# GNN message sending: casts as transpositions, wide picks, and one PSUM pool of 8 banks

## The reference

```python
msgs = edge_vals[:, None] * x[edge_col]              # x is layer-normed here
agg = segment_sum(msgs, edge_row, num_segments=n)
h = (1.0 + eps) * x + agg
h = bn_relu(h @ W1 + b1); h = bn_relu(h @ W2 + b2)   # batch norm over the nodes
x = x + h
H = gelu(layernorm(x) @ W1f + b1f)
probs = softmax(H @ Wg + bg); e = argmax(probs)
out = x + probs[e] * (H @ Wd[e] + bd[e])             # one expert per node
```

## Time and profile before

| | |
|---|---|
| three runs, median (lowest to highest) | 3251.73 us (3246.09 to 3256.91) |
| the profiled execution's own time | 3250.25 us |
| its span | 3248.4 us |
| mean granted clock of TensorE | 0.956 of 2.4 GHz |
| busy, share of the span | PE 88%, PEld 74%, DVE 74%, ACT 50%, POOL 25% |
| DMA | 710.52 MB, mean 219 GB/s |

### The profile page before, as it was taken

The page is one execution under the profiler, slowest core; times in us unless marked ns, Lnnn a source line. Parts: engine busy times, 40 slices in busy tenths (PEclk is TensorE's granted clock), DMA queues, the critical chain, the costliest instruction groups (busy, mean ns, idle before and its releaser), DMA issues. The chain is left out here.

```text
span 3248.4 us, 70401 instructions
## 1 busy us (share of the span) xinstructions
PE 2860.7 (88%) x20204; PEld 2392.9 (74%) x20205; DVE 2408.5 (74%) x5908; ACT 1618.7 (50%) x3203; POOL 823.2 (25%) x885
## 2 busy tenths in 40 slices
PE   4887678888888887999999999987999999599998
PEld 2333477777777776888888888755777777499998
DVE  8998967677777765888888888766666666666665
ACT  3664456566666663222222222575777777533332
POOL 4221045555555552000000000021222222122222
PEclk9888889999999998999999999998999999799999
DMA  2332077778777777999999999100344444566664
GB/s 56 106 115 74 20 261 291 279 283 306 290 292 283 284 288 298 330 335 333 345 332 327 333 329 332 49 0 26 131 157 178 155 174 159 215 211 211 214 214 135
DMA packets 214806, 710.52 MB, mean 219 GB/s; under 512 B 28495, under 2 KB 104313, under 8 KB 189514
## 3 DMA queue, kind: packets, MB, share of 16 engines
q1 hardware_dynamic: 130778, 405.55, 36.7%
q0 software_dynamic: 83952, 304.02, 24.1%
HBM read 383.91 MB, written 340.05 MB: 223 GB/s over the span
## 5 line engine op out<-in xcount | busy, mean ns | idle before, releaser
L1437 PE MATMUL coll_ps_sum<-coll_rows,coll_hot 128*128 128x256 f32 x2940 | 657.4, 380 | 23.5 <-DVE coll_hot L1372 23.2
L1088 PE MATMUL send_ps_msg<-send_parts,send_pick 128*128 128x256 f32 x3584 | 558.6, 300 | 108.1 <-ACT send_msg L1128 86.6
L1437 PEld LDWEIGHTS coll_ps_sum<-coll_rows,coll_hot 128*128 128x128 f32 x2940 | 550.1, 190 | 101.5 <-DVE coll_hot L1372 28.3
L1088 PEld LDWEIGHTS send_ps_msg<-send_parts,send_pick 128*128 128x128 f32 x3584 | 476.3, 198 | 129.8 <-DVE send_pick L991 78.3
L943 POOL DMA_INDIRECT messages<-send_msg,send_to x448 | 468.9, 1047 | 379.9 <-ACT send_msg L1128 235.9
L1128 ACT ACTIVATE send_msg<-send_ps_msg 128x1024 f32<-128x1024 f32 x448 | 454.1, 1027 | 221.7 <-PE send_ps_msg L1088 158.3
L991 DVE TENSOR_SCALAR send_pick<-send_ps_local,edges_down 128x512 fp32r<-128x512 f32 x448 | 334.2, 746 | 209.5 <-PE send_ps_local L1076 136.4
L1372 DVE TENSOR_SCALAR coll_hot<-coll_nodes,coll_rows 128x128 f32<-128x128 f32 x1470 | 393.4, 340 | 2.2 <-DMA coll_rows<-messages 0.8
L1491 ACT ACTIVATE nodes_hid<-coll_ps_turned 128x256 f32 (+1 forms) x98 | 37.5, 383 | 553.1 <-PE coll_ps_turned L1269 553.1
L1566 POOL CAST lin_x_hi<-lin_hT 128x1024 fp32r<-128x1024 f32 x25 | 29.2, 1168 | 940.1 <-ACT lin_hT L1702 887.4
L2033 DVE TENSOR_TENSOR gate_act_lo<-gate_act_h,gate_act_hi 128x512 fp32r<-128x512 f32 x200 | 141.7, 709 | 167.5 <-ACT gate_act_hi L1942 126.3
(11 more groups left out here) (335 smaller groups left out, 5887.2 us busy)
## 6 DMA issues: line engine op xcount, KB each, us to landing
coll_rows<-messages SPq DMA_DIRECT2D x98, 1300.0 KB, 7.3
coll_rows<-messages SPq DMA_DIRECT2D x98, 1170.0 KB, 7.3
exp_pay<-regions SPq DMA_DIRECT2D x105, 646.0 KB
send_window<-node_rows SPq DMA_DIRECT2D x112, 128.0 KB
node_rows<-sort_xn SPq DMA_DIRECT2D x25, 512.0 KB, 5.0
coll_own<-node_rows SPq DMA_DIRECT2D x98, 128.0 KB, 4.1
sort_xt<-in_x_dram SPq DMA_DIRECT2D x24, 512.0 KB, 4.3
layers_w<-in_x_dram SPq DMA_DIRECT2D x24, 384.0 KB
```

The costliest lines, as they stand in the source:

```text
L1088: ins = pe.matmul(ps_msg[:, q % 2, a, :], pick[:, q * RUN + a, :], parts[:, s % 2, part, :], start=(part == 0), stop=(part == 1))
L1437: ins = pe.matmul(ps_sum[:, s, 0:D], hot_of(s, j), features(u, j), start=(j == CX), stop=(j == CJ - 1))
```

## The change

Per group, TensorE no longer turns `local`; each of the 16 casts is a transposition of one column of `local`, repeated 128 times by a step of 0, in bf16, 8 to a call and one call to a bank. `pick` has two buffers and is made by two instructions of 1024 elements instead of four of 512. All of PSUM is one tensor of 8 banks; products, casts and sorted columns take them in turn. The order changes: sort and take run for group i+3, rows and slots for i+4. `parts` and `local` have 4 slots. localT, its clearing, ps_turned and their semaphores go.

```diff
-        pick = m.sb("pick", [P, QJ, P], F32R)
+        local = m.sb("local", [P, SLOTS, QJ], BF16)
+        pick = m.sb("pick", [P, 2, QJ, P], F32R)
-        parts = m.sb("parts", [P, 2, 2, D], F32R)
+        parts = m.sb("parts", [P, SLOTS, 2, D], F32R)
-        ps_found = m.ps("ps_found", [P, 512])
-        ps_turned = m.ps("ps_turned", [P, 512])
-        ps_local = m.ps("ps_local", [P, 2, RUN, P])
-        ps_msg = m.ps("ps_msg", [P, 2, RUN, D])
+        banks = m.ps("banks", [P, 8, 512])
+        PAIR_OF = (0, 4, 6, 2)
+        CAST_AT = (2, 0)
+        SORT_AT = 3
+        def bank(g, at):
+            return (4 * (g % 2) + at) % 8
+        def sums_of(s, q):
+            return banks[:, bank(s, PAIR_OF[q]):bank(s, PAIR_OF[q]) + 2, :].rearrange("p b (a f) -> p (b a) f", f=D)
+        def casts_of(s, h):
+            return banks[:, bank(s + 1, CAST_AT[h]), :].bitcast(BF16).rearrange("p (j m) -> p j m", m=P)
+        def found_of(u, first):
+            return banks[:, first if first is not None else bank(u + 1, SORT_AT), 0:SORTED]
...
+                def picks(i, s, h):
+                    if later(i, 2):
+                        dve.wait_ge(gathered, QS * (i - 1))
+                    dve.wait_ge(cast_done, 2 * i + h + 1)
+                    dve.tensor_scalar(pick[:, s % 2, h * QJ // 2:(h + 1) * QJ // 2, :], casts_of(s, h), k.down[:, 0:1], None,
                                       ALU.is_equal).then_inc(pick_ready, 1)
...
                 def group(i, s, turn):          # VectorE
+                        rest(i + 1, (s + 1) % SLOTS)
+                        rows_of(i + 4, s % 2)
+                        picks(i + 1, (s + 1) % SLOTS, 0)
+                        slots_of(i + 4, s % 2)
                         meta(i + 2, far, far % 2, turn if s + 2 < SLOTS else turn + 1)
+                        picks(i + 1, (s + 1) % SLOTS, 1)
...
+                def sort(i, s, first=None):
-                    if later(i, 1):
-                        pe.wait_ge(found_ready, i)
+                    if later(i, 4):
+                        pe.wait_ge(kept, QS * (i - 3) - 1)
+                def cast(i, s, h):
+                    if h == 0:
+                        pe.wait_ge(local_ready, i + 1)
+                    if later(i, 2):
+                        pe.wait_ge(kept, QS * (i - 1) - 1 if h == 0 else QS * (i - 1) + 1)
+                    elif later(i, 1) and h == 1:
+                        pe.wait_ge(kept, 1)
+                    for j in range(QJ // 2):
+                        n = h * QJ // 2 + j
+                        ins = pe.transpose(casts_of(s, h)[:, j, :], local[:, s, n:n + 1].to_broadcast([P, P]), k.ident16[:])
                 def gather(i, s, q):
                     if q == 0:
                         pe.wait_ge(rest_ready, i + 1)
+                        pe.wait_ge(pick_ready, 2 * i + 1)
+                        if later(i, 1):
+                            pe.wait_ge(kept, QS * i - 2)
+                        else:
+                            pe.wait_ge(found_ready, 2)
+                    if q == 1:
+                        pe.wait_ge(pick_ready, 2 * i + 2)
+                    if q == 2:
+                        if later(i, 1):
+                            pe.wait_ge(kept, QS * i)
+                        else:
+                            pe.wait_ge(found_ready, 3)
+                    if q == 3:
+                        if comes(i, 1):
+                            pe.wait_ge(pick_ready, 2 * i + 3)
+                        if comes(i, 3):
+                            pe.wait_ge(found_ready, i + 4)
...
                 def group(i, s, turn):          # TensorE
                     gather(i, s, 0)
+                        cast(i + 1, (s + 1) % SLOTS, 0)
+                        sort(i + 3, (s + 3) % SLOTS)
                     gather(i, s, 1)
                     gather(i, s, 2)
+                        cast(i + 1, (s + 1) % SLOTS, 1)
                     gather(i, s, 3)
...
-                    act.activation(localT[0:QJ, d, :], ps_turned[0:QJ, 0:P], ACT.Copy).then_inc(localT_ready, 1)
                 def group(i, s, turn):          # ScalarE
                         high(i + 1, (s + 1) % SLOTS, turn if s + 1 < SLOTS else turn + 1)
                     keep(i, s, turn, 0)
+                        take(i + 3, (s + 3) % SLOTS)
                     keep(i, s, turn, 1)
                     keep(i, s, turn, 2)
-                        take_turned(i + 2, s % 2)
                     keep(i, s, turn, 3)
```

More of the change, by code:

```diff
@@ L1009, in rest @@
                     dve.wait_ge(high_ready, i + 1)
-                    dve.tensor_tensor(parts[:, s % 2, 1, :], window[:, s, :], parts[:, s % 2, 0, :].bitcast(F32),
+                    dve.tensor_tensor(parts[:, s, 1, :], window[:, s, :], parts[:, s, 0, :].bitcast(F32),
                                       ALU.subtract).then_inc(rest_ready, 1)
@@ L1015, in group @@
                     steps.restart()
-                    near, far = (s + 1) % SLOTS, (s + 2) % SLOTS
+                    far = (s + 2) % SLOTS
                     if comes(i, 1):
[L1018 to L1021, removed]
+                        rest(i + 1, (s + 1) % SLOTS)
+                    if comes(i, 4):
+                        rows_of(i + 4, s % 2)
                     if comes(i, 1):
[L1023 to L1027, removed]
+                        picks(i + 1, (s + 1) % SLOTS, 0)
+                    if comes(i, 4):
+                        slots_of(i + 4, s % 2)
                     if comes(i, 2):
@@ L1036, in _ @@
                 meta(0, 0, 0, 0)
-                rest(0, 0)
[L1038 to L1044, removed]
+                picks(0, 0, 0)
+                picks(0, 0, 1)
+                rows_of(2, 0)
+                slots_of(2, 0)
+                meta(1, 1, 1, 0)
+                rest(0, 0)
+                rows_of(3, 1)
+                slots_of(3, 1)
                 all_groups(dve, group)
@@ L1082, in gather @@
                         pe.wait_ge(rest_ready, i + 1)
-                    pe.wait_ge(pick_ready, QS * i + q + 1)
-                    if q >= 2 or later(i, 1):
-                        pe.wait_ge(kept, QS * i + q - 1)
+                        pe.wait_ge(pick_ready, 2 * i + 1)
[15 more added lines that the diff above has]
+                            pe.wait_ge(found_ready, i + 4)
                     for a in range(RUN):
                         for part in range(2):
-                            ins = pe.matmul(ps_msg[:, q % 2, a, :], pick[:, q * RUN + a, :], parts[:, s % 2, part, :],
+                            ins = pe.matmul(sums_of(s, q)[:, a, :], pick[:, s % 2, q * RUN + a, :], parts[:, s, part, :],
                                             start=(part == 0), stop=(part == 1))
@@ L1094, in group @@
                     if comes(i, 1):
[L1095 to L1097 removed]
+                        cast(i + 1, (s + 1) % SLOTS, 0)
+                    if comes(i, 3):
+                        sort(i + 3, (s + 3) % SLOTS)
                     gather(i, s, 1)
[L1099 to L1100 removed]
                     gather(i, s, 2)
                     if comes(i, 1):
[L1103 to L1105 removed]
+                        cast(i + 1, (s + 1) % SLOTS, 1)
                     gather(i, s, 3)
[L1107 to L1112 removed]
+                sort(0, 0, 0)
+                sort(1, 1, 1)
                 cast(0, 0, 0)
                 cast(0, 0, 1)
[L1115 to L1117 removed]
+                sort(2, 2)
                 all_groups(pe, group)
@@ L1156, in group @@
                     keep(i, s, turn, 0)
-                    if comes(i, 2):
-                        take(i + 2, s % 2)
+                    if comes(i, 3):
+                        take(i + 3, (s + 3) % SLOTS)
                     keep(i, s, turn, 1)
                     keep(i, s, turn, 2)
-                    if comes(i, 2):
-                        take_turned(i + 2, s % 2)
                     keep(i, s, turn, 3)
-                take(0, 0)
-                act.wait_ge(localT_clear, 1)
-                take_turned(0, 0)
+                take(0, 0, 0)
+                take(1, 1, 1)
                 high(0, 0, 0)
-                take(1, 1)
-                take_turned(1, 1)
+                take(2, 2)
                 all_groups(act, group)
```

67 lines of the change are left out of this document (12 added, 55 removed).

## The result

The changed kernel takes **3291.47 us** (median of 4, 3287.03 to 3295.28), the kernel before 3248.91 beside it (4 runs): ratio 1.0133, 95% interval 1.0099 to 1.0168: slower by 1.3%. The forecast was 3117 us. In the profiled execution (span 3289.6 us) the split of the window starts 7.71 us apart ((1268.0 - 411.7)/111), where the earlier trace rows gave 7.40; 0.32 x 111 = 35 us of loss, in this stage.

What follows compares the result with a forecast made beforehand. Sending was taken as bound by a latency circle of gather, late signal, copy, gather over two buffers. TensorE's 5.62 us plus waits, clock and DMA gave 6.2 per group, not 7.40: 3250 - 133 = 3117 us, range 3062 to 3205.

Steps and rivals of the forecast that it cites:

- The prices of single instructions: Sending stage: casts 0.058 us each on TensorE, two picks of 1.25 us on VectorE, turning of the slots gone.
- Rivals 1 and 3: 1: repeated-column loads 0.11 us apart, 3195 us, chance 0.15. 3: transpositions don't overlap, 0.224 us each, 3372 us, 0.06.
- The clock that the prediction feared to lose by transpositions: Sending stage: casts might not count as activity, clock 0.96 to 0.85, period 6.8 us, time 3183 us; not taken.
- The stall of the products for `keep`: TensorE's wait for ScalarE's copy out of PSUM, 84.8 us before, was to fall to under 20 us.
- Needed: 1.40 + 1.03 + 0.1: Late signal plus copy before a gather reuses banks: 2.53 us needed, room 2.56 to 3.05, so the stall goes.
- 2.17 late: Picks 0 before gather 3: lateness plus 1.25 + 0.1 needs 3.52 us, room 3.05, so 0.47 short.
- the burst of short products: Casts and sorting on TensorE, around which other engines were said to see its completion late, 1.40 and 2.17 us.
- Rival 2: Lateness returns through casts 0, pick, gather 3, gather 0: 3.81 us plus lateness, 3215 to 3250 us, chance 0.11.
- 459/111 = 4.14 busy: GpSimd's busy time per group in sending; with about 0.3 us between issues, 5.3 us per group.
- What late is next: The wait of gather 3 for picks 0, 0.47 us short in a late group, named as the next late thing.
- become a neighbour: DMA engines in sending: 5.55 us of all engines per group, 6.03 to 6.3 at the best rates; only 0.1 added.

Runs made afterwards that it cites:

- k5: The changed kernel with GpSimd's four indirect DMAs per group replaced by plain DMAs of GpSimd to consecutive rows: 3091.19 us, 0.9525 of the kernel before.
- k11: The changed kernel with messages written by plain DMAs of SyncE, plus four indirect DMAs of GpSimd per group with 64-byte rows: 3327.77 us, ratio 1.0208.
- k2: The changed kernel with gather 3 writing one bank only, so the wait for `found` moves to gather 2 of the next group: 3306.58 us, ratio 1.0147.
- b3: A separate kernel: TensorE runs freely beside GpSimd's indirect DMAs at several spacings; 9.9 short products per us back to back, 27.8 at 2.7 us.
- b2: A separate kernel: signalled TensorE rounds beside plain or indirect DMAs; the answering copy starts 0.03 us after the sorting beside plain, 16.7 us beside indirect ones.
- k9: The changed kernel with a small memset, waited for, after each of GpSimd's indirect DMAs in the sending stage: 3406.94 us, ratio 1.0456.
- k12: The changed kernel with plain message DMAs of GpSimd, plus two indirect DMAs of 64-byte rows per group: 3118.74 us, ratio 0.9566.

## Why the prediction was wrong

- *The prices of single instructions* were right: casts as transpositions 0.056 us from start to start (0.058 taken), picks 1.278 us (1.25 taken; the slope of 0.53 in its upper bound of 1.28 stands in no row), `send_localT` gone. Rivals 1 and 3 are out. The clock that the prediction feared to lose by transpositions was 1.00 with them where the pauses were gone (k5), and 0.93 in the changed kernel, not the 0.85 of its estimate.
- *The stall of the products for `keep`* shrank, to 32.8 us, but did not go.
- **The step that failed** is the one under the waits, "Needed: 1.40 + 1.03 + 0.1", and "2.17 late" in the next: a lateness read from one group, laid at the door of "the burst of short products", and carried over as a constant. It is held by GpSimd's indirect DMAs (k5, k11), it lasts as long as they run in a row, and the change made that row longer, from three to four: the sorting's signal came 4.6 us late in the group above, 2.78 instead of 1.60 on average. Rival 2 asked for 3.6 us and was given 0.11, for the wrong cause, and its range ended at 3250 us; its own edge, picks before gather 3, did not carry the wait (6.7 us in all for `send_pick`).
- *GpSimd* stood in the sum as "459/111 = 4.14 busy", 5.3 us with what lies between, an engine with room. Its four DMAs (3 x 1.3 us between starts), the hold behind the last and the way back through take, copy and issue are the period: from the first DMA at 1002.34 to the next first at 1010.44 it is 8.1 us, on average 7.7. This circle is read from the rows; that it alone sets the period no run isolates.
- *What late is next* missed the wait for `found` before gather 3, the largest named one after. Taking it away alone (k2) shows that it would not have mattered.
- *The DMA engines* "become a neighbour": in the changed kernel they do not (0.71 busy), and with plain writes they are the bound. There the change is worth 0.9549 - 0.9525 = 0.0024, 8 us, not 133, since before then runs at 0.98 of the DMA engines already. That the time forecast, 3117, is near k5's 3091 is luck: it is what a kernel without indirect DMAs takes, and most of it would not have been the change's merit.

## What to carry to other kernels

When engines see TensorE's products late, look first at what GpSimd's queue does in that time: a signal that moves with an indirect DMA isn't TensorE's property, and must not stand in a sum as a constant. Before pricing buffers against such a lateness, replace the suspect by something plain of the same bytes and time both kernels; two such runs here would have shown both the 195 us and the 8. And when the wait that the profile names can be taken away without effect, the kernel is in a circle: count its way round, not its longest edge.

## What the runs showed that was not expected

- Indirect DMAs of GpSimd hold TensorE's completion signals, up to 16.7 us in a row, and slow short products from 28 to 10 per us, 4.6 where they are held without a break (b3, full rows). Signals were late with rows of 4160, 256 and 64 bytes alike (b2, k11); beside plain DMAs of GpSimd and SyncE none was.
- A held signal comes mostly 0.72, 0.96 or 1.4 us behind the one before it. DMAs with 2.28 us or 3.56 between starts held nothing, those with 2.7 did: why is open.
- Indirect DMAs 2.1 us apart instead of 1.3 take the sorting's lateness from 2.78 to 0.10 us (k9), and two short ones per group, each followed by a plain one, leave 0.05 (k12).
- With plain writes the DMA engines are 0.99 busy at 377 GB/s (k5); with indirect ones they were left at 0.71 and 274.
